# State space layer: step-size groups over both side banks, turned inputs in the other bank, output products and gate products at other steps

## The reference

```python
xz = xs @ in_proj_w.T                       # 384 -> 2 x 768
xin, z = jnp.split(xz, 2, axis=-1)
xin = silu(conv1d_4(xin) + conv_b)          # depthwise, 4 taps
dt, Bm, Cm = jnp.split(xin @ x_proj_w.T, [24, 40], axis=-1)
dt = softplus(dt @ dt_proj_w.T + dt_proj_b)
h_t = exp(dt_t * A) * h_{t-1} + dt_t * B_t * x_t     # per channel and state
y_t = sum_s h_t[s] * C_t[s]
y = (y + xin * D) * silu(z)
out = layernorm(y @ out_proj_w.T)
```

## Time and profile before

| | us |
|---|---|
| median of three runs | 5354.77 |
| lowest, highest | 5343.97, 5362.83 |
| the profiled execution | 5347.93 |
| its span | 5346.1 |

### The profile page before, as it was taken

The page is one execution under the profiler, slowest core; times in us unless marked ns, Lnnn a source line. Parts: engine busy times, 40 slices in busy tenths (PEclk is TensorE's granted clock), DMA queues, the critical chain, the costliest instruction groups (busy, mean ns, idle before and its releaser), DMA issues.

```text
span 5346.1 us, 78656 instructions
## 1 busy us (share of the span) xinstructions
PE 4686.3 (88%) x28623; PEld 3835.5 (72%) x28623; DVE 4381.3 (82%) x4965; ACT 3070.4 (57%) x6391; POOL 2970.7 (56%) x3552
## 2 busy tenths in 40 slices
PE   4888888888888888888888886779998899999999
PEld 2666666666666666666666665446877799999999
DVE  1999999999999999999999999677677765665555
ACT  3777777777777777777777774333332223333333
POOL 3776777777777777777777775456554520000000
PEclk8999999999999999999999999889797988999999
DMA  2001000001000001000000001110201021112110
GB/s 78 1 13 33 10 10 10 10 11 35 10 10 10 10 11 35 10 10 10 10 10 10 10 5 44 44 32 20 92 20 41 26 72 53 54 51 60 45 60 29
DMA packets 96933, 148.64 MB, mean 28 GB/s; under 512 B 5748, under 2 KB 93604, under 8 KB 96548
## 3 DMA queue, kind: packets, MB, share of 16 engines
q1 hardware_dynamic: 96548, 143.63, 8.4%
HBM read 101.00 MB, written 42.61 MB: 27 GB/s over the span
## 4 chain that ended last, share of the span: by engine, by line
PE 50%; issue 15%; DVE 15%; POOL 12%; ACT 7%; DMA 1%; POOLq 0%; DVEq 0%; SPq 0%; ACTq 0%
PE pw L1776 8%; PE pw L1763 6%; PE pw L462 6%; PE pw L451 6%; DVE a_h L744 5%; POOL a_dBT L882 4%; PE ps L413 3%; PE ps L353 3%; DVE b_cv L1393 3%; PE ps L373 2%; DVE a_acc L763 2%; PE ps L1763 2%; POOL a_xin L834 2%; POOL a_acc L894 2%; PE pw L1176 2%
## 5 line engine op out<-in xcount | busy, mean ns | idle before, releaser
L744 DVE TENSOR_TENSOR_SCAN a_h<-a_dA,pw 128x771 f32<-128x771 f32 x1152 | 2015.7, 1752 | 125.6 <-PE pw L451 124.6
L600 ACT ACTIVATE a_dA<-a_dt,a_Aneg 128x384 f32<-128x384 f32 x2304 | 1345.5, 607 | 155.0 <-DVE a_h L744 150.1
L462 PEld LDWEIGHTS pw<-g_ident,a_h 128*128 128x128 f32 x6912 | 786.6, 142 | 619.8 <-DVE a_acc L763 267.1
L882 POOL TENSOR_SCALAR a_dBT<-a_dtxT,a_BC 128x768 f32<-128x768 f32 x1152 | 1026.2, 909 | 300.7 <-PE pw L451 216.6
L462 PE MATMUL pw<-g_ident,a_h 128*128 128x128 f32 x6912 | 983.1, 279 | 227.5 <-DVE a_acc L763 158.1
L451 PE MATMUL pw<-g_ident,a_dBT 128*128 128x128 f32 x6912 | 958.9, 276 | 4.8 <-POOL a_dBT L882 4.8
L763 DVE SCALAR_TENSOR_TENSOR a_acc<-pw,a_BC,a_acc 128x768 f32<-128x768 f32 x912 | 915.3, 1004 | 52.5 <-PE pw L462 48.1
L451 PEld LDWEIGHTS pw<-g_ident,a_dBT 128*128 128x128 f32 x6912 | 806.5, 143 | 6.5 <-POOL a_dBT L882 5.5
L834 POOL TENSOR_TENSOR a_xin<-a_xin,a_tm 128x384 f32<-128x384 f32 x432 | 433.3, 1003 | 34.2 <-ACT a_tm L521 9.0
L1887 DVE TENSOR_TENSOR d_hf<-d_hf,d_wb 128x384 f32<-128x384 f32 x288 | 159.1, 557 | 312.4 <-ACT d_hf L1819 300.2
L894 POOL TENSOR_TENSOR a_acc<-a_acc,a_tm 128x768 f32<-128x768 f32 x168 | 307.4, 1830 | 171.1 <-ACT a_tm L614 170.2
(11 more groups left out here) (228 smaller groups left out, 9377.7 us busy)
## 6 DMA issues: line engine op xcount, KB each, us to landing
d_wb<-cw SPq DMA_DIRECT2D x24, 768.0 KB, 5.7
a_xs<-in_x SPq DMA_DIRECT2D x24, 576.0 KB, 3.9
x<-a_xs SPq DMA_DIRECT2D x24, 576.0 KB, 3.0
b_x<-x SPq DMA_DIRECT2D x24, 576.0 KB, 4.4
b_xs<-x SPq DMA_DIRECT2D x24, 576.0 KB, 5.0
e_xs<-x SPq DMA_DIRECT2D x24, 576.0 KB, 3.8
out<-e_xs SPq DMA_DIRECT2D x24, 576.0 KB, 5.8
a_sx<-in_x SPq DMA_DIRECT2D x54, 192.0 KB, 2.3
```

Of the source, the lines that this page charges most:

```text
L462: t = e.transpose(m["pw2"][:, c * 128:(c + 1) * 128], m[f"a_h{g % 2}"][:, c // 2, first_col(c) + tb * 128:first_col(c) + (tb + 1) * 128], ...
L600: e.activation(dA[:, first_col(c):first_col(c) + T], m[f"a_dt{k % 2}"][:, c, :], ACT.Exp, scale=m["a_Aneg"][:, c, n:n + 1]).then_inc(s["a_ ...
L744: e.tensor_tensor_scan(m[f"a_h{g % 2}"][:, p % 3, :], m[f"a_dA{pi % NDA}"][:], m[f"pw{pi % 2}"][:, COL:COL + PAIR], 1.0, ALU.mult, ALU.add ...
L882: t = e.tensor_scalar(m[f"a_dBT{g % 2}"][:, tb, :], m[f"a_dtxT{o}"][:, tb, :], m[f"a_BC{o}"][:, tb, n:n + 1], 1.0, ALU.mult, ALU.mult)
```

## The change

Step sizes' groups 1, 3 and 5 go to D and 0, 2, 4 stay in S, 1.1 steps apart from 58.4 in place of 0.8 from 58. All six turned inputs go from S to D. Output products come up to a step earlier, x-projection, B and C and their readers 0.6 to 0.7 later, norm groups 8 to 10 steps later, gate products at steps of their own, 1.2 apart. ScalarE's readers and GpSimd's follow. In the third chunk of an image 16 small loads instead of 13 stand ahead of store and load. No instruction is added or removed.

```diff
-O_AT, O_GAP, LN_AT = (18.8, 30, 40.2), (1.8, 1.6, 1.1), (29.5, 39.8, 47)
-G_AT = (60, 62.5, 66)
-T_AT = (78.6, 79.8, 81, 85.6, 86.6, 87.6)
-Z_AT = (63.5, 67.5, 71.5, 75, 82, 88.8)
+O_AT, O_GAP, LN_AT = (18.4, 29.2, 39.2), (1.8, 1.6, 1.1), (29.1, 39, 46.3)
+V_AT = (58.4, 59.5, 60.6, 61.7, 62.8, 63.9)
+G_AT = (68.1, 72.1, 76.1)
+T_AT = (80.2, 81.1, 82, 86, 86.9, 87.8)
+Z_AT = (64.8, 68.8, 72.8, 76.8, 82.8, 89.6)
+Z_GAP = 1.2
...
     for j in range(6):
-        yield 47 + 1.2 * j
+        yield 47.7 + 1.2 * j
         if j == 0:
             D.claim("v_dt3", k + 1)
...
-    yield 56.8
+    yield 57.4
     S.claim("a_bc", k + 1)
...
     for i in range(6):
-        yield 58 + 0.8 * i
-        S.claim("a_v", 6 * k + i + 1)
+        yield V_AT[i]
+        (D if i % 2 else S).claim("a_v", 6 * k + i + 1)
...
-        e.matmul(ps[:, 0:T], m["a_Wdt3"][:, i * 128:(i + 1) * 128], m["a_dt3"][:], start=True, stop=True).then_inc(s["pe_V"], 1)
+        e.matmul((pd if i % 2 else ps)[:, 0:T], m["a_Wdt3"][:, i * 128:(i + 1) * 128], m["a_dt3"][:], start=True, stop=True).then_inc(s["pe_V"], 1)
...
-            S.claim("a_dtx", 6 * k + 3 * hf + tb + 1)
+            D.claim("a_dtx", 6 * k + 3 * hf + tb + 1)
...
-            yield at + 1.3 * kk
+            yield at + Z_GAP * kk
...
-    yield 54.5
+    yield 55.2
     w.wait_ge("pe_X", k + 1)
...
-    yield 57.3
+    yield 57.9
...
-        yield 58.4 + 0.8 * i
+        yield V_AT[i] + 0.4
...
-    yield 64.5
+    yield 65.3
     w.wait_ge("a_v", 6 * (k + 1))
     e.activation(dt[:], dt[:], ACT.Exp, scale=-1.0).then_inc(s["a_sp"], 1)
-    yield 67
+    yield 67.5
     w.wait_ge("a_sp", 2 * k + 1)
...
-        yield at + 3
+        yield at + 2 * Z_GAP + 0.4
         w.wait_ge("pe_Z", 6 * k + i + 1)
...
-    yield 55.3
+    yield 56
     w.wait_ge("pe_X", k + 1)
...
-        yield 69 + 2 * i
+        yield 69.5 + 2 * i
...
-        yield 70 + 2 * i
+        yield 70.5 + 2 * i
...
-        for i in range(more - 5):
+        for i in range(more - 2):
             stats(b + 1, i)
...
-        for i in range(max(0, more - 5), more):
+        for i in range(max(0, more - 2), more):
             stats(b + 1, i)
```

More of the change, by code:

```diff
@@ L397, in pre_pe @@
             yield T_AT[3 * hf + tb]
-            S.claim("a_dtx", 6 * k + 3 * hf + tb + 1)
+            D.claim("a_dtx", 6 * k + 3 * hf + tb + 1)
             w.wait_ge("p_dtx", 6 * k + 3 * hf + 3)
             for c in range(3):
-                t = e.transpose(ps[:, c * 128:(c + 1) * 128], m["a_raw"][:, 3 * hf + c, 3 + tb * 128:3 + (tb + 1) * 128], ident[:])
+                t = e.transpose(pd[:, c * 128:(c + 1) * 128], m["a_raw"][:, 3 * hf + c, 3 + tb * 128:3 + (tb + 1) * 128], ident[:])
             t.then_inc(s["pe_T"], 1)
@@ L547, in pre_act @@
         w.wait_ge("a_exp", 3 * PAIRS * (k - 1))
-        e.activation(dt[:, i, :], ps[:, 0:T], ACT.Abs, bias=pv[:, i, 5:6])
-        e.activation(raw[:, i, 3:T + 3], ps[:, 0:T], ACT.Relu, bias=pv[:, i, 5:6]).then_inc(s["a_v"], 1)
-    yield 64.5
+        pi = pd if i % 2 else ps
+        e.activation(dt[:, i, :], pi[:, 0:T], ACT.Abs, bias=pv[:, i, 5:6])
+        e.activation(raw[:, i, 3:T + 3], pi[:, 0:T], ACT.Relu, bias=pv[:, i, 5:6]).then_inc(s["a_v"], 1)
+    yield 65.3
     w.wait_ge("a_v", 6 * (k + 1))
     e.activation(dt[:], dt[:], ACT.Exp, scale=-1.0).then_inc(s["a_sp"], 1)
-    yield 67
+    yield 67.5
     w.wait_ge("a_sp", 2 * k + 1)
@@ L561, in pre_act @@
         hf, tb = divmod(u, 3)
-        e.activation(m[f"a_dtxT{o}"][:, tb, hf * T:(hf + 1) * T], ps[:, 0:T], ACT.Copy).then_inc(s["a_dtx"], 1)
+        e.activation(m[f"a_dtxT{o}"][:, tb, hf * T:(hf + 1) * T], pd[:, 0:T], ACT.Copy).then_inc(s["a_dtx"], 1)
 def silu_gate(e, m, w, k):
```

## The result

The kernel after takes 5374.85 us (median, 5372.14 to 5377.46), the kernel before 5355.79 (5343.97 to 5365.40). The ratio is 1.0034, 95% interval 1.0022 to 1.0046. The forecast was 5357 in a range of 5282 to 5394, so the time is in the range, 18 us above the forecast. It is just above the 5339 to 5371 that the prediction called "the same": slower by 0.3%, clear of the noise by the interval.

A forecast was written before the change was run, and what follows sets the result against it. VectorE, busy 82% of the span, was taken as the bound. Sixteen chunks +18, three like chunk 4 +8, statistics -15, opening -6, chunk 0 +1: +6 on 5347.9 gives 5354, put at 5357; range 5282 to 5394 with rivals.

The forecast's parts named there:

- Steps 0 to 46: First half of a chunk: TensorE's late output and in-projection products at steps 19 and 33 cost 1.3 us a chunk.
- Steps 46 to 58: Earlier last output group and later x-projection cut the stretch from 18.15 to 15.2 us, saving 2.95 a chunk.
- Steps 58 to 70: First gate product's read comes behind Ln, stalling step 69: 19.4 us between scans, a cost of 2.7 a chunk.
- The alternation itself is worth nothing there: Steps 58 to 70: step-size groups alternating between two banks gain nothing, as each still has to pass ScalarE.
- Steps 70 to 95: Turned inputs no longer share S with gate products; waits at steps 89 and 90 go, saving 1.1 a chunk.
- Clock: TensorE's 2.7 us stand before step 69's gate product slows its clock: 1.2 us a chunk, ends 0 and 1.6.
- Statistics: Three chunks with statistics: small loads ahead of the store remove VectorE's waits, saving 5 us in each.
- Opening: Before the first scan: two banks for step-size groups and fewer bank handovers save 6 us.
- Chunk 0 and the chunks with group sums: Chunk 0 costs 1 us with its own gate stall; group-sum chunks predicted at +3.5 for three.
- The first: Rival 1: no gate stall at step 69, ScalarE reads in time or two banks help; 5290, chance 0.25.
- The second: Rival 2: slow clock every chunk after the stall, steps 73, 77 and 83 cost another 1.0; 5388, chance 0.18.
- The third and fourth: Rival 3: small loads don't keep up, 5372, chance 0.07. Rival 4: moves cancel, clock stays up, 5348, chance 0.08.

The follow-up runs named there:

- one-bank run: Kernel after with the gate read ahead of Ln, plus all six step-size groups in bank S: 5363.96 us, ratio to before 1.0027.
- combined kernel: Kernel after with Ln behind the first gate read, first two output groups at old times, one turned input per odd step, group sums later: 5232.45 us.
- kernel with two more moves: Combined kernel with ScalarE's second step-size pair due at 60.2 instead of 59.9 and group sums at step 75: 5224.94 us, ratio to before 0.9737.

## Why the prediction was right or wrong

**Steps 0 to 46: right.** +1.3 was forecast; the scan of step 46 comes 65.34 us after that of step 0, before 64.05. The waits are 0.83 at step 19 and 0.6 at step 33. Undone alone it gives 1.29 back. What the sum lacked is that TensorE, once late, carries 0.6 of it past step 46.

**Steps 46 to 58: right.** 15.2 forecast, 15.18 measured (990.24 to 1005.42); before 18.15.

**Steps 58 to 70: right in mechanism, 0.4 too high.** 19.4 forecast, 18.98 measured. The wait at step 61, which was to stay at 0.88, is 1.29. The stall is where it was said to be, 2.39 of TensorE and 1.87 of VectorE in place of 2.7 and 2.5, and the experiment with Ln behind the read shows that the order alone makes it.

**"The alternation itself is worth nothing there": wrong.** It is worth 1.75 a chunk, 38 to 50 us. The step that failed is the reason given, that each group has to pass ScalarE anyway. That is so, and ScalarE's six pairs with what stands between them are only 0.2 us longer with one bank (10.43 and 10.25). But VectorE waits for TensorE, and TensorE's own queue was left out of this judgement: with one bank it stands 1.14 to 1.59 us at a handover, with VectorE's transposes behind. The sum of this stretch was not harmed, because it priced the kernel after and not the difference.

**Steps 70 to 95: wrong, by 1.3 a chunk, 28 us in all.** A saving of 1.1 was forecast, with two norm groups (1.0) moved in; the stretch went from 33.0 to 34.2. The wait at step 90 did go. What failed is the reckoning of steps 83 and 87: it counted two turned inputs, a gate product and a read as 1.9 us of TensorE (1.6 to 1.9 at step 87, to be borrowed), and did not ask where ScalarE's read stands on its own queue. The second turned input needs the bank of the first. The first is complete at 1046.34, but ScalarE, with the gate read and a decay ahead, starts to read it only at 1047.03 and is done at 1047.51; so TensorE stands 1.23 us. This was in the same table of due times from which the stall at step 69 was read. One input to a step gave 2.0 back (34.2 to 32.3).

**Clock: over-sized.** 1.2 a chunk was forecast, as three quarters of 1.6. The slow stretch costs 1.4, but came in six chunks for the gap at step 69, and besides at step 88 of three and at step 18 of chunk 12: 0.7 in the mean of the thirteen ordinary chunks. So an ordinary chunk has errors of -0.4 (steps 58 to 70), +1.3 (70 to 95) and -0.5 (clock), which leave about +0.3 (1.45 where 1.15 was forecast). That so much of the 28 us was paid back is luck, and with it that the total came out within 18.

**Statistics: right** (-5.3 in place of -5), and given alone to the kernel before 7.9, where there is no gate stall: the two waits that were named (6.7) and small ones behind them. **Opening: right** (-5.0 for -6); the one-bank run has its first scan 2.5 later than its pair, so of the 4 us given to the banks there about 2.5 hold, as far as one trace of each tells. The first scan comes at 117.4 to 121.8 in the eight traces with two banks, at 126.1 to 130.4 in the three of the kernel before and the runs built on it; so the gain is real, its size uncertain by some 4 us.

**Chunk 0 and the chunks with group sums: under-sized.** In chunk 0 +4.2 where +1 was written: its own stall is 2.71 us and comes with the slow clock; with the gate read first the chunk is 3.2 shorter. The chunks with group sums got 2.9 in place of 1.15. In chunk 9 VectorE waited 1.24 for the sums and 0.60 ahead of the scan of step 90; after, it waits 0.66 for them, then 1.35 ahead of that scan and 0.50 at step 91, besides 0.79 and 1.03 at steps 84 and 87, and the clock falls at step 88. The sums share bank D with the turned inputs, which were moved there; that this is the cause is not shown.

**Later layers:** "0 with 3 either way" was too narrow. Traces of identical code differ by up to 9.2.

**Rivals.** The first (no stall, 5290) did not happen, but its price can be set beside a run: without the stall 5313.69, a gain of 61 where 68 was worked out. The second (slow clock in every chunk and nothing left to borrow, 5388) is half there: VectorE's wait at step 69 is 1.87, under the 2 us on which it rested, and there are new waits at steps 83 to 87, for another reason. The third and fourth did not occur.

## What to carry to other kernels

On a queue that works in order, a due time is a place in line: before moving one, write out each engine's order on both sides of its longest instructions. A read of 0.5 us put behind a 2.2 us instruction cost some 60 us here, and was mended by one number. And price a wait with the next one behind it: of the 3.6 us won at the x-projection 1.2 were lost again at the next bank handover. The other way round, all the repairs together (142 us against the change) brought more than the 118 that they bring one by one, since no gap was left at which the clock fell.

## What the runs showed of the hardware

**Equal gaps, unequal clocks.** TensorE stands 2.39 us before the same instruction in almost every chunk of two kernels. In one (after) the granted clock falls behind it in six chunks, in the other (the first two output groups at their old times) in 21. Each fall cost 1.4 us.

**A tiny instruction of VectorE waits for GpSimd.** With the group sums read at step 76, while GpSimd makes the step sizes, one 128x3 product of VectorE took 0.98 us; at step 92 of the combined kernel, while GpSimd stands idle, it takes 0.16. VectorE's timeline and GpSimd's in the kernel with two more moves, then both in the combined one:

```profile
1378.70 0.16 DVE L683 TENSOR_SCALAR a_gs<-ps 128x6 f32<-128x6 f32 x1
1378.89 0.98 DVE L685 TENSOR_TENSOR a_gs<-a_gs 128x3 f32<-128x3 f32 x1
```

```profile
1378.86 1.00 POOL L848 TENSOR_TENSOR a_raw<-a_dt,a_xin 128x384 f32<-128x384 f32 x1
```

```profile
1404.73 0.16 DVE L685 TENSOR_TENSOR a_gs<-a_gs 128x3 f32<-128x3 f32 x1
```

```profile
1405.38 0.87 POOL L864 TENSOR_TENSOR a_sc<-a_gs,g_mhalf 128x3 f32<-128x3 f32 x1 [1.59 <-DVE a_gs L689]
```

The slow one ends at 1379.87, with GpSimd's (1379.86), which had begun 0.03 before it. The same is seen in all three chunks with group sums (0.96, 0.98, 0.98 and 0.16 each). That is why moving the group sums won nothing: their five small instructions take 2.0 us there and 0.8 at the old place, which is 1.2 of the 1.4 that VectorE waits less. The Trainium skill (SBUF — State Buffer, SBUF: two separate sides) describes a pair of ports that VectorE, with two operands in SBUF, and GpSimd, where it reads SBUF, can only hold one at a time, for a whole instruction. The trace agrees: the product has both operands in `a_gs`, and it lasts until GpSimd's instruction ends.
